# Causal attention: the bias of heads 2 and 3 through ScalarE and GpSimd in steps with maxima, and biased exponentials one step later

## The reference

```
q, k, v = heads(x @ Wq + bq), heads(x @ Wk + bk), heads(x @ Wv + bv)
q = q * cos + rotate_half(q) * sin;  k = k * cos + rotate_half(k) * sin
att = (einsum('bhid,bhjd->bhij', q, k) + bias[None]) * (1 / sqrt(8))
att = where(causal, att, -inf);  att = softmax(att)
y = einsum('bhij,bhjd->bhid', att, v)  ->  y @ Wp + bp
```

## Time and profile before

| | us |
|---|---|
| median of 3 runs | 3416.59 |
| lowest, highest | 3409.17, 3417.78 |
| the profiled execution | 3408.68 |
| its span | 3406.9 |
| PE busy | 3023.7 (89%) |
| DVE busy | 2440.1 (72%) |
| ACT busy | 1802.7 (53%) |
| POOL busy | 851.4 (25%) |

### The profile page before, as it was taken

One profiled execution on the slowest core, in us unless ns is written; L12 is line 12 of the kernel. 1 busy time (PEld: TensorE's weight loads), 2 busy tenths in 40 slices (PEclk: granted clock), 3 DMA queues, 4 the chain that ended last, 5 costly groups with the idle time before them and its releaser, 6 DMA issues. The chain is left out here.

```text
span 3406.9 us, 61884 instructions
## 1 busy us (share of the span) xinstructions
PE 3023.7 (89%) x24429; PEld 1641.8 (48%) x24469; DVE 2440.1 (72%) x5485; ACT 1802.7 (53%) x3298; POOL 851.4 (25%) x809
## 2 busy tenths in 40 slices
PE   4878679998799999998899989798998898898999
PEld 3435456666322222223566657476775222333677
DVE  8898688777699999994877743745336888884433
ACT  2223347777477777775778743133222466776211
POOL 0333147765100000002966700101203111212000
PEclk8898889999699999999999989898999699998899
DMA  1065221110420000001211110002002300000100
GB/s 54 9 160 138 64 64 34 37 37 11 153 81 2 1 1 1 1 1 28 63 28 35 31 31 1 12 18 75 25 1 83 103 32 1 35 2 1 48 1 13
DMA packets 77879, 129.20 MB, mean 38 GB/s; under 512 B 12772, under 2 KB 52616, under 8 KB 77384
## 3 DMA queue, kind: packets, MB, share of 16 engines
q1 hardware_dynamic: 77592, 125.25, 13.0%
HBM read 77.39 MB, written 34.19 MB: 33 GB/s over the span
## 5 line engine op out<-in xcount | busy, mean ns | idle before, releaser
L2039 ACT ACTIVATE AR<-ps 128x1024 f32<-128x1024 f32 (+2 forms) x756 | 717.7, 995 | 275.3 <-PE ps L1940 207.9
L2126 DVE TENSOR_REDUCE AR<-ps 128x1 f32<-128x512 f32 x1296 | 808.4, 682 | 43.0 <-PE ps L1909 42.0
L1940 PE MATMUL ps<-AR 32*128 32x512 bf16 (+3 forms) x4992 | 536.0, 378 | 6.4 <-ACT AR L2039 4.2
L1909 PE MATMUL ps<-AR 32*128 32x512 bf16 (+3 forms) x1664 | 478.1, 398 | 41.3 <-DVE AR L2126 13.7
L1957 PE MATMUL ps<-AR 128*32 128x512 f32 (+3 forms) x3328 | 439.8, 602 | 4.9 <-ACT AR L2044 3.1
L2535 PEld LDWEIGHTS ps<-AR 128*128 128x128 f32 x3072 | 362.9, 192 | 60.5 <-issue 47.5
L2694 DVE SCALAR_TENSOR_TENSOR X<-ps,AR,X 128x128 f32<-128x128 f32 x512 | 143.6, 344 | 343.5 <-PE ps L2535 343.2
L1909 PEld LDWEIGHTS ps<-AR 32*128 32x128 bf16 x1664 | 120.1, 92 | 548.5 <-DVE AR L2126 410.3
L2535 PE MATMUL ps<-AR 128*128 128x128 f32 x3072 | 363.0, 275 | 0.0
L2510 PE MATMUL ps<-XT,AR 128*128 128x512 f32 x672 | 307.7, 594 | 0.1
L205 POOL TENSOR_TENSOR rs<-rs,halves 128x4 f32<-128x4 f32 x48 | 49.5, 1031 | 841.7 <-DVE rs L197 841.7
(11 more groups left out here) (326 smaller groups left out, 5004.2 us busy)
## 6 DMA issues: line engine op xcount, KB each, us to landing
AR<-AR SPq DMA_DIRECT2D x124, 128.0 KB, 2.3
band<-AR SPq DMA_DIRECT2D x32, 450.0 KB, 5.1
AR<-band SPq DMA_DIRECT2D x32, 448.0 KB, 5.1
AR<-in_c_rot SPq DMA_DIRECT2D x64, 128.0 KB, 2.2
AR<-in_L3f_w SPq DMA_DIRECT2D x30, 256.0 KB, 5.6
rows_KA<-AR SPq DMA_DIRECT2D x32, 128.0 KB, 2.4
AR<-scr_bias SPq DMA_DIRECT2D x32, 128.0 KB, 3.1
AR<-in_L2f_w SPq DMA_DIRECT2D x30, 128.0 KB, 2.9
```

The costliest lines, as they stand in the source:

```text
L1909: e.matmul(g.bank[b][:, 0:w], QA[rows, q, 128 * i:128 * i + 128], KA[rows, q, 512 * first:512 * first + w], start=way != "kept", stop=True ...
L1940: t = e.matmul(g.bank[h][:, lo:512], K[32 * h:32 * h + 32, q, 128 * kt:128 * kt + 128], Q[32 * h:32 * h + 32, q, queries], start=y == 0, s ...
L2039: e.activation(dst[:, :, lo:512], src[:, :, lo:512], ACT.Exp, scale=self.scale).then_inc(*s.up("exp" if u else "left", k, i, *((1,) if u e ...
L2126: e.tensor_reduce(o, g.bank[b][:, 0:w], AXX, ALU.max).then_inc(*s.up("reduced", k, n, h, st, kc))
```

## The change

The steps with both a near range and maxima in one of their slots are put into a set, `pooled`. In them DVE no longer adds a bias for heads 2 and 3: ACT copies the biased columns of banks 2 and 3 to a new buffer NV in SBUF, POOL adds the bias there, and ACT takes the exponential from NV. In the near steps that are not pooled DVE still adds, but writes the sum to NV, from which ACT takes the exponential. Banks 2 and 3 are so released by the copy (or DVE's addition) and the exponential of the columns beyond, no longer by the whole exponential. The biased exponentials from NB, and in pooled steps those from NV, are moved: where the next step is near too, they are issued behind the first copy of that step. The values wait for the later of them. "max_rows" is moved behind "values", in both attention stages.

```diff
         if causal:
             self.BF, self.BN = g.near_bias
             self.NB = ar.f32(2, 2, 256)
+            self.NV = ar.f32(2, 2, 256)
@@ closers
+    def closers(self, i, n, kt):
+        near = self.near_cols(n, kt)
+        if not near:
+            return (("exp", i, 1),)
+        if i in self.pooled:
+            return (("near", i, 1), ("exp", i, "rest")) if near[1] < 512 * self.rounds[n][1] + 512 else (("near", i, 1),)
+        return (("biased", i), ("exp", i, "rest")) if near[1] < 512 * self.rounds[n][1] + 512 else (("biased", i),)
@@ lay_plan
+            if any(slots) and self.near_cols(n, kt):
+                self.pooled.add(i)
             for u in range(2):
                 for x in slots[u]:
                     self.plan_max(*x)
-                self.plan.append(("score", i, n, kt, u, self.hold(2 * u, ("exp", i, 1) if u else ("left", i)) + self.hold(2 * u + 1)))
+                self.plan.append(("score", i, n, kt, u, self.hold(2 * u, *(self.closers(i, n, kt) if u else (("left", i),)))
+                                  + self.hold(2 * u + 1)))
             self.plan.append(("step", i, n, kt))
             for x in slots[2]:
                 self.plan_max(*x)
-            if self.rows_due:
-                self.plan_rows_max(self.rows_due.pop(0))
...
                 if pk == last_kt[pn]:
                     finish_due.append(pn)
+            if self.rows_due:
+                self.plan_rows_max(self.rows_due.pop(0))
@@ tensor, "values"
                 if self.near_cols(n, kt):
-                    e.wait_ge(*s.at("exp", k, i, 0))
+                    e.wait_ge(*s.at("exp", k, i, 1 if i in self.pooled else 0))
@@ scalar, "step"
                         t = e.activation(nb, src[:, :, first:end], ACT.Copy)
                         t.then_inc(*s.up("near" if end < 512 else "left", k, i))
+                        if i and self.near_cols(*self.steps[i - 1]):
+                            self.near_exp(e, s, i - 1)
                         if end < 512:
                             e.activation(dst[:, :, end:512], src[:, :, end:512], ACT.Exp, scale=self.scale).then_inc(
                                 *s.up("left", k, i))
                         continue
+                    if u and i in self.pooled:
+                        e.wait_ge(*s.at("scored", k, i, 1))
+                        e.activation(self.NV[:, i % 2, :, 0:end - first], src[:, :, first:end], ACT.Copy).then_inc(
+                            *s.up("near", k, i, 1))
+                        if end < 512:
+                            e.activation(dst[:, :, end:512], src[:, :, end:512], ACT.Exp, scale=self.scale).then_inc(
+                                *s.up("exp", k, i, "rest"))
+                        continue
                     if u and near:
                         e.wait_ge(*s.at("biased", k, i))
-                    else:
-                        e.wait_ge(*s.at("scored", k, i, u))
+                        if end < 512:
+                            e.activation(dst[:, :, end:512], src[:, :, end:512], ACT.Exp, scale=self.scale).then_inc(
+                                *s.up("exp", k, i, "rest"))
+                        e.activation(dst[:, :, first:end], self.NV[:, i % 2, :, 0:end - first], ACT.Exp,
+                                     scale=self.scale).then_inc(*s.up("exp", k, i, 1))
+                        continue
+                    e.wait_ge(*s.at("scored", k, i, u))
...
-                if near:
-                    e.wait_ge(*s.at("near_biased", k, i))
-                    dst = self.PB[:, 2 * kt % 4, :].rearrange("p (a b) -> p a b", a=2)
-                    e.activation(dst[:, :, first:end], nb, ACT.Exp, scale=self.scale).then_inc(*s.up("exp", k, i, 0))
+                if near and (i + 1 == len(self.steps) or not self.near_cols(*self.steps[i + 1])):
+                    self.near_exp(e, s, i)
@@ near_exp
+        e.wait_ge(*s.at("near_biased", self.k, i))
+        e.activation(dst[:, :, a - 512 * qc:z - 512 * qc], self.NB[:, i % 2, :, 0:z - a], ACT.Exp, scale=self.scale).then_inc(
+            *s.up("exp", self.k, i, 0))
+        if i in self.pooled:
+            dst = self.PB[:, (2 * kt + 1) % 4, :].rearrange("p (a b) -> p a b", a=2)
+            e.wait_ge(*s.at("near_biased", self.k, i, 1))
+            e.activation(dst[:, :, a - 512 * qc:z - 512 * qc], self.NV[:, i % 2, :, 0:z - a], ACT.Exp,
+                         scale=self.scale).then_inc(*s.up("exp", self.k, i, 1))
@@ vector, "step"
-            if what == "step" and self.near_cols(x[1], x[2]):
+            if what == "step" and self.near_cols(x[1], x[2]) and x[0] not in self.pooled:
...
-                e.tensor_tensor(y, y, self.BF[:, 4 * gr + 2:4 * gr + 4, a - 128 * kt:z - 128 * kt], ALU.add).then_inc(
-                    *s.up("biased", k, i))
+                e.tensor_tensor(self.NV[:, i % 2, :, 0:z - a], y, self.BF[:, 4 * gr + 2:4 * gr + 4, a - 128 * kt:z - 128 * kt],
+                                ALU.add).then_inc(*s.up("biased", k, i))
@@ gpsimd, "step"
+                if i in self.pooled:
+                    nv = self.NV[:, i % 2, :, 0:z - a]
+                    e.wait_ge(*s.at("near", k, i, 1))
+                    e.tensor_tensor(nv, nv, self.BF[:, 4 * gr + 2:4 * gr + 4, a - 128 * kt:z - 128 * kt], ALU.add).then_inc(
+                        *s.up("near_biased", k, i, 1))
```

More of the change, by code:

```diff
@@ L1604, in lay_plan @@
         causal, rounds, last_kt = self.causal, self.rounds, self.last_kt
-        self.plan, self.left, self.rows_made = [], {b: () for b in range(8)}, set()
+        self.plan, self.left, self.rows_made, self.pooled = [], {b: () for b in range(8)}, set(), set()
         self.ring = self.closed = 0
@@ L1744, in wait_left @@
                 e.wait_ge(*s.at("exp", k, *key))
+            if what == "biased":
+                e.wait_ge(*s.at("biased", k, *key))
+            if what == "near":
+                e.wait_ge(*s.at("near", k, *key))
     def rot_name(self, c):
@@ L2055, in scalar, with near_exp @@
             e.activation(g.XT[:, chunk(c)], g.bank[c % 2], ACT.Copy).then_inc(*s.up("xt", k, c, "out"))
+    def near_exp(self, e, s, i):
+        n, kt = self.steps[i]
+        (a, z), qc = self.near_cols(n, kt), self.rounds[n][1]
+        dst = self.PB[:, 2 * kt % 4, :].rearrange("p (a b) -> p a b", a=2)
+        e.wait_ge(*s.at("near_biased", self.k, i))
[6 more added lines that the diff above has]
+                         scale=self.scale).then_inc(*s.up("exp", self.k, i, 1))
     def last_step(self, n):
```

## The result

The changed kernel takes 3441.1 us (median of 4 runs, 3435.8 to 3443.5) against 3416.0 for the one before: ratio 1.0076, 95% interval 1.0063 to 1.0089, some 25 us slower. The forecast was 3428, slower, with 8 in 10 between 3400 and 3446. Its profiled execution took 3439.2 us, a span of 3437.5.

A forecast was written before the change was run, and what follows sets the result against it. No engine was full; DVE set the pace in near steps of causal attention. 14.2 - 4.0 - 7.5 + 0 - 3.0 + 3.4 + 8.0 = +11.1 us gave 3428 us from the median, 8 in 10 between 3400 and 3446.

The forecast's parts named there:

- the chain: Consecutive near steps: score, ACT's copy, late biased exponentials, values, next score form a closed loop, 3.49 us in one kind.
- the forecast's own: The forecast case for the whole kernel: 3428 us, own range 3414 to 3440, chance 0.36.
- the rival that had loops and clock both worse: Causal attention: ACT's queue becomes the bound, each block brings two half-clock stretches; +24 us, 3441, chance 0.15.
- Part 1: Near steps with maxima: 62 additions leave DVE, 36.8 us; ACT gains 39.8 us; POOL's second addition stays hidden.
- Part 2: Blocks of near steps: the later exponentials close a loop from one score to the next; +14.2 us.
- part 7: Clock: one more half-clock stretch behind each block of near steps and the tail; +8 us (0 to +16).
- Part 3: First near steps of eight blocks: loop not yet closed, DVE relieved; -0.5 us each, -4.0 (0 to -8).
- Part 4: max_rows behind values: PE's waits for POOL nearly go, -7.5 us (0 to -12); other attention stage 0 (-3 to +3).
- Part 5: Twelve near steps of the first rounds: the loop stays under the step's time; -3 us (-8 to +3).
- Part 6: Tail, 14 near steps without maxima: DVE keeps the bias, one exponential in the loop; +3.4 us (0 to +6).

The follow-up runs named there:

- experiment 6: The changed kernel with no step pooled, plus one more exponential into an unread buffer: in the chain 3468.1 us, at the end of its own step 3421.3 us.
- experiment 7: The changed kernel with the exponential from NB back in its own step, that from NV still late: 3396.5 us, again 3398.6 us.
- kernel 1: The kernel before with only max_rows moved behind the values: 3398.0 us, again 3402.1 us.
- kernel 5: The changed kernel with no step pooled and no late exponentials, keeping DVE's sum in NV and max_rows moved: 3406.2 us.
- kernels 3: The changed kernel with the biased exponentials back at the end of their own step, bias still through POOL: 3415.9 us.
- kernel 4: The changed kernel with no step pooled: DVE adds the bias into NV, exponentials of heads 0 and 1 still late: 3416.7 us.
- the twin: kernel 4 with one more exponential into an unread buffer, at the end of its own step: 3421.3 us.
- kernel 2: The changed kernel with max_rows back ahead of the values: 3445.6 us.
- kernel 8: The changed kernel with the first product of the second half of the scores issued three more times in near steps: 3435.9 us.
- the longer chain: kernel 4 with one more exponential into an unread buffer, just ahead of the late one: 3468.1 us.

## Why the prediction was right, and where it was off

The mechanism and the sign were right, and so was the chain's length (3.38 us measured for the loop reckoned at 3.49, whose listed terms add to 3.48). The sum was +11 and the runs say +25. 3441 lies in the wide range but just outside the forecast's own, 3414 to 3440; it is the number of the rival that had loops and clock both worse. That rival's clock came true, its other half didn't: ACT's queue is no bound, ACT is busy 9.5 of 12.5 us in the second cut and waits for scores. By the prediction's parts, with sizes from one profiled execution each, which lie 30.6 us apart where the medians lie 25:

- **Part 1** (DVE's bias leaves, POOL's second addition is hidden): right but for the count, 56 for 62, and the sizes: in the stage DVE is busy 24.5 us less, not 36.8, and ACT 27 us more, not 39.8. ACT's waits for POOL are 3 us.
- **Part 2** (loops, +14.2): the seven cuts went up by 10.9 us against 10.4 reckoned: +0.7, +2.3, +1.2, +2.0, 0.0, +2.4, +2.2. Experiments 6 and 7 show the chain as the cause by moving one link in and out. Steps 72 to 83 went up by 12.6 instead of 3.8; their clock is 0.61, so I put the 8.8 us more down to part 7.
- **Part 3** (first near steps, -4.0): -3.4 for the eight, of it -2.2 in steps 99 and 115, which also hold max_rows.
- **Part 4** (max_rows, -7.5 and 0 for the other stage): mis-sized and misplaced. Alone it gains 11 to 16 us, of it 4.0 in the other stage, outside the +3 to -3 I allowed; in the changed kernel 4.5 by the medians, 4.6 of it in the other stage.
- **Part 5** (first rounds, -3): -0.1; with one exponential out of the loops (experiment 7) the same steps fall by 6 us, at a higher clock. **Part 6** (tail, +3.4): +1.1, +0.8 and +0.7, together 2.5.
- **Part 7** (clock, +8) is the step that failed in size: some +20, an estimate, above the 0 to +16 that I allowed. From the rows, half-clock time is twice the missing share: 2 x 0.11 x 496.8 = 109 us before and 2 x 0.16 x 529.5 = 169 us after. What it costs is read from the far steps 104 to 114, whose work is the same in both: 3.5 us more for about 10 us more at half clock, a third (in the two executions of experiment 7, 4.4 us for 12). So 60 us cost 20. I had taken one stretch more for each block of near steps. What came was not more stretches so much as longer ones: half of the 60 us are the one of 37.5 us in steps 75 to 84, in place of two of 3.4.

Without the clock the measured parts make 10.9 + 3.8 - 3.4 - 4.5 - 0.1 + 2.5 = +9 us, less than the 10 that the prediction held to be tellable. That the kernel came out clearly slower hangs on the term that was called the least sure.

Over the kernels a longer stage goes with a lower clock: 484 us at 0.91 (kernel 7, one exponential out of the loop), 489 at 0.89 (kernel 1), 494 at 0.89 (before) and at 0.87 (kernel 5), 505 and 509 at 0.86 (kernels 3 and 4), 510 at 0.87 (the twin), 527 and 530 at 0.84 (the changed kernel and kernel 2), 529 at 0.86 (kernel 8), 560 at 0.77 (the chain made longer). This order alone doesn't say which makes which. That PE's pauses in near steps lower the clock is supported by the longer chain with 0.77 beside its twin with 0.87; the one attempt to break the link (experiment 8) didn't settle it. What exactly decides the clock stays open.

## What to carry to other kernels

Before an instruction is moved behind another, write down what that other waits for, and whether its releaser in turn waits, in program order, behind a consumer of the moved one: that closes a loop, and its length, once it is longer than what the engines need, is the step. The first link may look cheap: here one late exponential cost 10 us (kernel 5 to 4), the next one 51 (kernel 4 to the longer chain) or 45 (kernel 7 to the changed one). Relief of the busiest engine is worth nothing inside such a loop; moving only the part that needs the time (here the exponential behind the later addition) kept the cover and took 0.52 us out of the loop. A piece that waits on one queue should stand behind work that is ready anyway, and its gain must be looked for in every stage that shares the code.

## What was not expected of the hardware

The same far steps took 27.5 to 28.5 us with the clock at 0.96 to 1.00, 30.8 at 0.84 and 31.9 to 32.9 at 0.77 to 0.81, over all kernels here, and one kernel showed both ends. Half the clock did not double the matmuls' drawn time, as the prediction took it: in the kernel before, a score product of 512 columns is drawn 0.37 us at full clock and 0.63 at half, between 2840 and 2850 us. In the changed kernel 37.5 us went by at half clock with no pause of PE over 1.5 us. An exponential of 128 x 512 from SBUF is drawn 0.62 us long but sets the next ACT instruction back by 0.52, in the chain of experiment 6 exactly by that.
